# One transposition, one copy and one row transfer for two column groups of maxima

## The chip, the cores and the metric

The kernel runs on 1 core of one Trainium2 chip. The metric is device time in microseconds (us) of one launch. Before the change it is 2338.07 us, the median of three runs (2335.86 to 2340.33).

## The reference

The inputs are x (64 batches of 128 tokens, 512 wide), a context of 64 x 128 x 128, two gates and the weights of a mixture of experts. What is computed, with the expert part cut to a line:

```
q, k, v = layernorm(x), ctx, ctx            # 32 query heads of 16, 8 key/value heads, 4 query heads per key head
scores  = einsum('bkgsd,bktd->bkgst', qh, kh) / 4
weights = softmax(scores, axis=-1)
x = x + tanh(g_xattn) * (weights @ v)
x = x + tanh(g_ffn) * moe(layernorm(x))     # 32 experts, top 4, capacity 64, and a shared expert of 1408 columns
```

The change touches only the maximum that the softmax takes off each row of scores.

## The kernel before

Everything is written out by hand: five engine programs (PE, ACT, DVE, POOL, SP), each in its own order, tied by counting semaphores. The first stage is the attention. `iterations` runs a `body(B)` on every engine for B = 0 to 67; seven first and the last ones are written out, those between stand in a loop of two bodies. Each body has four steps, c = 0 to 3, one for a column group: eight query heads, four of each of two key heads.

A column group goes through these places. Batches are in flight together, so one step serves several of them:

- `q_cols` (PE, L623): four transpositions into `p_tq`; ACT copies them to `qt` (L425).
- First pass (PE, L704, `p_max`): the scores of group c of batch B, four matmuls. DVE reduces them over the keys to eight negated maxima per token in `negmax` (L562).
- Maxima (PE, L712): one transposition of `negmax` (128 x 8) into `p_mt` (8 x 128), ACT copies it to `mt` (L464), and SP sends it with two transfers, one per key head, into row 0 and row 64 of `qt` (L265), where it becomes one more term of the dot product. In the kernel before, this stands at the end of a step, behind the first pass, for the group of the step before: (B, c - 1), or (B - 1, 3) at c = 0. PE's step is: second pass, other work, `q_cols`, first pass, maxima.
- Second pass (PE, L663, `p_exp`): group c of batch B - 1 with the maxima's row in it, two matmuls, one step of the next body. It waits for the row's semaphore `mrow_in` and for the exponential before. ACT takes the exponential (L441).
- Then `pv` (PE, L639) at c = 2 (B - 1, first half) and c = 0 (B - 2, second half), its copy `pv_evac` (ACT, L430, `ot_sb`), the transpositions `o_cols` (L649), the division by the sums and the residual (DVE, L529, L542), a second layer norm (`xn`, L506), its transposition (PE, L673, `p_pv`, at c = 1 for B - 3), and router logits at c = 2 (L686).

`p_pv` is one bank used in turn by `pv`, by the transposed keys (`k_cols`, L615, at c = 3) and by the transposed `xn` (L673), so each of these waits until ACT has emptied it. SP's queue, in order, does the row transfers of every step, and between them at c = 0 the loads of `xres` and the store of `xn` rows, at c = 1 the loads of x and the context for B + 3, the values and the store of `xn` columns, at c = 2 the store of x2. In every second body SP also loads a slice of the shared expert's weights and ACT and POOL split it (`wgu_h`, L467, at the end of the even body; `wgu_l`, L402).

The second stage, from about 745 us on, is the mixture of experts and is not touched.

Of the kernel before, what the change touches and what calls it, by code (L numbers as in the profile page):

```python
# [14 lines left out]
F32 = mybir.dt.float32  # L15
F32R = mybir.dt.float32r
# [8 lines left out]
G = NH // NKV  # L25
# [73 lines left out]
def build(nc, x, ctx_in, g_xattn, g_ffn, Wr, Wg, Wu, Wd, Wsg, Wsu, Wsd, Wse, out):  # L99
# [7 lines left out]
    with stack:  # L107
# [29 lines left out]
        with ExitStack() as scope:  # L137
# [15 lines left out]
            xn = [sb(f"xn_{i}", [128, E]) for i in range(2)]  # L153
            xnT = [sb(f"xnT{i}", [128, KC, 128]) for i in range(2)]
            wr = sb("wr", [128, KC, NE + 1])
            negmax = [sb(f"negmax{i}", [128, 8]) for i in range(2)]
            mt = [sb(f"mt{i}", [8, 128], F32R) for i in range(2)]
            st1, st2 = sb("st1", [128, 6]), sb("st2", [128, 6])
            mv1 = [sb(f"mv1_{i}", [128, 2]) for i in range(2)]
            mv2 = [sb(f"mv2_{i}", [128, 2]) for i in range(2)]  # L160
# [18 lines left out]
            p_tq = ps("p_tq", [128, 512])  # L179
            p_pv = ps("p_pv", [128, 512])  # L180
            p_ot = ps("p_ot", [128, 512])
            p_mt = ps("p_mt", [8, 128])

            x_in = [sem(f"x_in{i}") for i in range(2)]
            kv_in = [sem(f"kv_in{i}") for i in range(2)]
# [53 lines left out]
            @block.sync  # L239
            def _(sp):  # L240
                sp.dma_start(wr[:, :, 0:NE], Wr.rearrange("(k p) e -> p k e", p=128)).then_inc(wr_in, 16)
                sp.dma_start(wr[:, :, NE:NE + 1], Wse.rearrange("(k p) e -> p k e", p=128),
                             allow_slow_non_contiguous=True).then_inc(wr_in, 16)
                sp.dma_start(gx[:, :], g_xattn.rearrange("(a n) -> a n", a=1).to_broadcast([128, 1])).then_inc(g_in, 16)
                sp.dma_start(gf[:, :], g_ffn.rearrange("(a n) -> a n", a=1).to_broadcast([128, 1])).then_inc(g_in, 16)

                def load_in(b):
                    wait(sp, qraw_done, b.n - 1)
                    sp.dma_start(xs[b.par][:, :], x_t[b.n]).then_inc(x_in[b.par], 16)
                    wait(sp, ks_done, b.n - 1)  # L250
                    sp.dma_start(kv[b.par][:, :], ctx_in[b.n]).then_inc(kv_in[b.par], 16)

                def body(B):
                    if isinstance(B.n, int) and B.n == 0:
                        load_in(B)
                        load_in(B + 1)
                        load_in(B + 2)
                    for c in range(NC):
                        m = (B - 1, 3) if c == 0 else (B, c - 1)
                        if m[0].ok:  # L260

                            b, cc = m
                            wait(sp, mt_done, 4 * b.n + cc + 1)
                            for g2 in range(2):
                                sp.dma_start(qt[b.par][64 * g2:64 * g2 + 1, cc, :].bitcast(F32),  # L265
                                             mt[cc % 2][4 * g2:4 * g2 + 4, :].bitcast(F32)).then_inc(mrow_in[cc % 2], 16)
                        if c == 0:
                            if (B - 1).ok:
                                wait(sp, x2_done, (B - 1).n - 1)
                                sp.dma_start(xres[(B - 1).par][:, :], x_t[(B - 1).n]).then_inc(xres_in[(B - 1).par], 16)  # L270
                            if (B - 3).ok:
                                b = B - 3
                                wait(sp, xn_done, b.n + 1)
                                sp.dma_start(xn_dram[bass.ts(b.n, 128), 0:E], xn[b.par][:, :]).then_inc(xn_out[b.par], 16)
                        if c == 1:
                            if (B + 3).ok:
                                load_in(B + 3)
                            if B.ok:
                                wait(sp, pv_mm, 2 * (B.n - 1))
                                if isinstance(B.n, int) and B.n < 2:  # L280
                                    sp.wait_ge(pads, 4)
                                sp.dma_start(vals[B.par][:, :, 0:D], ctx_in[B.n].rearrange("t (g d) -> t g d", d=D)).then_inc(v_in[B.par], 16)
                            if (B - 3).ok:
                                b = B - 3
                                wait(sp, xnT_done, b.n + 1)
                                alone(sp, spare_s)
                                sp.dma_start(xT_dram[:, :, bass.ts(b.n, 128)].rearrange("k p t -> p k t"), xnT[b.par][:, :, :]).then_inc(xnT_out[b.par], 16)
                        if c == 2 and (B - 2).ok:
                            b = B - 2
                            wait(sp, x2_done, b.n + 1)  # L290
                            sp.dma_start(out_rows[bass.ts(b.n, 128), :], x2[b.par][:, :]).then_inc(x2_out[b.par], 16)
                    if weights_load(B):

                        wait(sp, wlo_done, B.pair)
                        alone(sp, spare_s)
                        for w, src in enumerate((Wsg, Wsu)):
                            sp.dma_start(wst[:, w, :, :], src.rearrange("(k p) n -> p k n", p=128)[:, :, bass.ts(B.pair, WCH)]).then_inc(wst_in, 16)
                    if isinstance(B.n, int) and B.n == LAST:
                        for i in range(2):
                            sp.wait_ge(xnT_out[i], 32)  # L300
                        sp.dma_start(x_first[:, :, :], xT_dram[:, :, 0:TILE].rearrange("k p t -> p k t")).then_inc(x_first_in, 16)
                iterations(sp, body)
                sp.wait_ge(x_first_in, 16)
                for s in (x2_out, xn_out, xnT_out):
                    for i in range(2):
                        sp.wait_ge(s[i], 16 * (NB // 2))
# [102 lines left out]
            def _(act):  # L409
# [22 lines left out]
                def body(B):  # L432
# [3 lines left out]
                    for c in range(NC):  # L436
                        b = B - 1
                        if b.ok:
                            act.wait_ge(p2_mm, 4 * b.n + c + 1)
                            wait(act, pv_mm, 2 * (b.n - 1) + c // 2 + 1)  # L440
                            nc.scalar.activation(probs[c][:, :], p_exp[:, :, :].rearrange("p a b -> p (a b)"), ACT.Exp,  # L441
                                                 scale=float(D) ** -0.5).then_inc(exp_done, 1)
                        if c == 1 and (B - 3).ok:
                            b = B - 3
                            act.wait_ge(xnT_mm, b.n + 1)
                            wait(act, xnT_out[b.par], 16 * b.half)
                            wait(act, lg_mm, b.n - 1)
                            nc.scalar.activation(xnT[b.par][:, :, :].rearrange("p k t -> p (k t)"), p_pv[:, :], ACT.Copy).then_inc(xnT_done, 1)
# [7 lines left out]
                            q_evac(B, c + 1)  # L456
                        if c == 3 and (B + 1).ok:
                            q_evac(B + 1, 0)
                        b, cc = (B - 1, 3) if c == 0 else (B, c - 1)
                        if b.ok:  # L460

                            act.wait_ge(mt_mm, 4 * b.n + cc + 1)
                            wait(act, mrow_in[cc % 2], 32 * (2 * b.n + cc // 2))
                            nc.scalar.activation(mt[cc % 2][:, :], p_mt[:, :], ACT.Copy).then_inc(mt_done, 1)  # L464
                    if weights_split(B):
                        act.wait_ge(wst_in, 32 * (B.pair + 1))
                        nc.scalar.activation(w_cols(wgu_h, B.pair), wst_cols, ACT.Copy).then_inc(whi_done, 1)  # L467
# [3 lines left out]
            def _(dve):  # L471
# [59 lines left out]
                def body(B):  # L531
# [4 lines left out]
                    for c in range(NC):  # L536
# [21 lines left out]
                            x2_stats = stats(x2[B.par][:, :], st2)  # L558
                        if B.ok:
                            dve.wait_ge(p1_mm, 4 * B.n + c + 1)  # L560
                            wait(dve, mt_mm, 4 * B.n + c - 1)
                            nc.vector.tensor_reduce(negmax[c % 2][:, :].rearrange("p (g i) -> p i g", i=G),  # L562
                                                    p_max[:, :, :].rearrange("p a (h g t) -> p (a h) g t", g=2, t=128),
                                                    AX.X, ALU.max, negate=True).then_inc(max_done, 1)
                        if c == 0:
# [38 lines left out]
            def _(pe):  # L604
# [47 lines left out]
                def body(B):  # L652
# [3 lines left out]
                    for c in range(NC):  # L656
                        b = B - 1
                        if b.ok:

                            pe.wait_ge(mrow_in[c % 2], 32 * (2 * b.n + c // 2 + 1))  # L660
                            wait(pe, exp_done, 4 * b.n + c)
                            for g2 in range(2):
                                last = mm(p_exp[:, g2, :], kt[b.par][:, c, 128 * g2:128 * g2 + 128], qt[b.par][:, c, :],  # L663
# [27 lines left out]
                            o_cols(B - 2, 1)  # L691
                        if c == 3 and (B - 1).ok:
                            o_cols(B - 1, 0)
                        if c < 3 and B.ok:
                            q_cols(B, c + 1)
                        if c == 3 and (B + 1).ok:
                            q_cols(B + 1, 0)
                        if B.ok:
# [5 lines left out]
                                last = mm(p_max[:, i // 2, 256 * (i % 2):256 * (i % 2) + 256], qt[B.par][:, c, 128 * i:128 * i + 128],  # L704
                                          kt[B.par][:, c, :], start=True, stop=True)
                            last.then_inc(p1_mm, 1)
                        b, cc = (B - 1, 3) if c == 0 else (B, c - 1)
                        if b.ok:

                            pe.wait_ge(max_done, 4 * b.n + cc + 1)  # L710
                            wait(pe, mt_done, 4 * b.n + cc)
                            last = tr(p_mt[:, :], negmax[cc % 2][:, :], ident[:, :])  # L712
                            last.then_inc(mt_mm, 1)
                iterations(pe, body)


# [503 lines left out]
```

## Time and profile before

| what | value |
|---|---|
| median of three runs | 2338.07 us |
| the profiled execution's own time | 2336.49 us |
| its span (first to last instruction) | 2334.7 us |
| first stage | to about 745 us |
| PE busy, whole span | 98% |
| granted TensorE clock, mean | 0.996 |
| row transfers `qt<-mt` | 512, 2 KB each |

The span is what the profile's rows are measured in, from its first instruction; the execution's time is 1.8 us longer. In a timeline a row is: start, duration, engine, line, what is written from what, count, and in brackets the idle time before and who ended it. Matmuls are pipelined: each lasts longer than the distance to the next start, so the price of one is that distance and not its duration.

### The profile page before, as it was taken

Reading aid. Unit: us, or ns where it says so; the run is one execution under the profiler, and the core shown is the slowest. Engines: PE = TensorE matmul, PEld = TensorE weight load, DVE = VectorE, ACT = ScalarE, POOL = GpSimd, SP = SyncE. Lnnn points to the kernel's source line nnn. Section 1 sums busy time; section 2 is a strip of 40 time slices with the busy share of each in tenths; the row PEclk is TensorE's granted clock in tenths of the full one; section 3 lists DMA queues with packets and bytes.
Section 4 is the critical chain, followed back from the end, with each engine's and each line's share of the span. In section 5 each row is a group of like instructions: output and inputs, shape, how many; then the busy total and the mean of one; then the engine's idle time right before and its main releaser. Section 6 shows DMA issues by size and latency. Waiting matters only on the chain.

```text
span 2334.7 us, 41674 instructions
## 1 busy us (share of the span) xinstructions
PE 2298.7 (98%) x12545; PEld 1775.1 (76%) x12545; DVE 1159.6 (50%) x2218; ACT 799.2 (34%) x1440; POOL 595.6 (26%) x1395
## 2 busy tenths in 40 slices
PE   7999999999998999999999999999999999999999
PEld 5777777777775877787777877777777777777777
DVE  6999999999996842332222323233222232323232
ACT  6888888888885110110101101011010100101010
POOL 5677677667663100000000000000000000000100
PEclk9999999999998999999999999999999999999999
DMA  3555555545545132232222232212322123222411
GB/s 82 137 146 141 137 143 141 140 135 145 143 130 172 21 105 92 69 112 83 83 79 67 94 101 83 79 63 90 111 83 79 63 79 104 84 82 82 141 66 43
DMA packets 271248, 235.15 MB, mean 101 GB/s; under 512 B 122337, under 2 KB 198113, under 8 KB 271202
## 3 DMA queue, kind: packets, MB, share of 16 engines
q1 hardware_dynamic: 266850, 221.90, 31.6%
q0 software_dynamic: 4352, 12.65, 1.9%
q8 instruction: 27, 0.44, 0.1%
q14 instruction: 19, 0.16, 0.0%
HBM read 161.88 MB, written 71.57 MB: 100 GB/s over the span
## 4 chain that ended last, share of the span: by engine, by line
PE 67%; DVE 1%; DMA 0%; issue 0%; DVEq 0%; POOLq 0%
PE acc L1126 7%; PE p_u L1142 7%; PE p_u L1144 7%; PE p_u L1143 7%; PE acc L1127 7%; PE acc L1128 7%; PE p_g L1142 7%; PE p_g L1144 7%; PE p_g L1143 7%; PE p_x L1174 2%; PE p_y L1161 2%; PE p_x L1161 2%; PE p_x L1152 0%; DMA rows<-out_dram 0%; PE p_y L1167 0%; DVE rows L1106 0%
## 5 line engine op out<-in xcount | busy, mean ns | idle before, releaser
L1060 DVE TENSOR_TENSOR act_f<-p_u,act_f 128x512 f32<-128x512 f32 x176 | 121.7, 692 | 984.7 <-PE p_u L1144 984.6
L965 ACT ACTIVATE act_f<-p_g 128x512 f32<-128x512 f32 x176 | 105.3, 598 | 1215.9 <-PE p_g L1144 1194.8
L562 DVE TENSOR_REDUCE negmax<-p_max 128x8 f32<-128x1024 f32 x256 | 312.5, 1221 | 56.5 <-PE p_max L704 54.1
L1126 PE MATMUL acc<-wd_h,hh 128*128 128x512 f32 x704 | 279.9, 398 | 0.0
L1142 PE MATMUL p_u<-xh,wgu_h 128*128 128x512 f32 x704 | 274.5, 390 | 4.0 <-DVE act_f L1060 4.0
L1142 PE MATMUL p_g<-xh,wgu_h 128*128 128x512 f32 x704 | 276.0, 392 | 0.0
L1127 PE MATMUL acc<-wd_l,hh 128*128 128x512 f32 x704 | 274.7, 390 | 0.0
L1128 PE MATMUL acc<-wd_h,hl 128*128 128x512 f32 x704 | 274.7, 390 | 0.0
L1144 PE MATMUL p_g<-xh,wgu_l 128*128 128x512 f32 x704 | 274.5, 390 | 0.0
L1143 PE MATMUL p_g<-xl,wgu_h 128*128 128x512 f32 x704 | 274.4, 390 | 0.0
L1144 PE MATMUL p_u<-xh,wgu_l 128*128 128x512 f32 x704 | 274.4, 390 | 0.0
L1143 PE MATMUL p_u<-xl,wgu_h 128*128 128x512 f32 x704 | 274.3, 390 | 0.0
L441 ACT ACTIVATE probs<-p_exp 128x1024 f32<-128x1024 f32 x256 | 259.6, 1014 | 26.9 <-PE p_exp L663 17.2
L704 PE MATMUL p_max<-kt,qt 128*128 128x256 f32 x1024 | 185.1, 303 | 1.5 <-DVE negmax L562 1.5
L663 PE MATMUL p_exp<-qt,kt 128*128 128x512 f32 x512 | 182.5, 438 | 2.2 <-DMA qt<-mt 2.1
L425 ACT ACTIVATE qt<-p_tq 128x512 fp32r<-128x512 f32 x256 | 151.4, 591 | 59.5 <-PE p_tq L623 58.0
L1126 PEld LDWEIGHTS acc<-wd_h,hh 128*128 128x128 f32 x704 | 132.3, 188 | 47.5 <-DVE hl L1066 13.0
L623 PEld LDWEIGHTS p_tq<-ident,qs 128*128 128x128 f32 x1024 | 120.4, 147 | 58.8 <-ACT qt L425 45.3
L623 PE MATMUL p_tq<-ident,qs 128*128 128x128 f32 x1024 | 161.8, 281 | 2.8 <-POOL qs L364 1.8
L922 POOL DMA_INDIRECT eo<-out_dram,cur_tok x32 | 31.0, 968 | 504.6 <-DMA out_dram<-rows 408.1
L1142 PEld LDWEIGHTS p_u<-xh,wgu_h 128*128 128x128 f32 x704 | 132.2, 188 | 32.2 <-DVE act_f L1060 4.9
L1128 PEld LDWEIGHTS acc<-wd_h,hl 128*128 128x128 f32 x704 | 132.3, 188 | 27.9
(142 smaller groups left out, 3616.7 us busy)
## 6 DMA issues: line engine op xcount, KB each, us to landing
ew<-in_L_ffn_Wg_dram SPq DMA_DIRECT2D x32, 704.0 KB, 6.1
ew<-in_L_ffn_Wu_dram SPq DMA_DIRECT2D x32, 704.0 KB, 7.7
xs<-in_x_dram SPq DMA_DIRECT2D x64, 256.0 KB, 2.7
xres<-in_x_dram SPq DMA_DIRECT2D x64, 256.0 KB, 2.9
out_dram<-x SPq DMA_DIRECT2D x64, 256.0 KB, 2.0
xn_rows<-xn SPq DMA_DIRECT2D x64, 256.0 KB, 3.0
xn_cols<-xnT SPq DMA_DIRECT2D x64, 256.0 KB, 2.6
rows<-out_dram SPq DMA_DIRECT2D x16, 1024.0 KB, 5.2
```

The costliest lines, as they stand in the source:

```text
L425: nc.scalar.activation(qt[b.par][:, c, :], p_tq[:, :], ACT.Copy).then_inc(tq_done, 1)
L441: nc.scalar.activation(probs[c][:, :], p_exp[:, :, :].rearrange("p a b -> p (a b)"), ACT.Exp, scale=float(D) ** -0.5).then_inc(exp_done, 1)
L562: nc.vector.tensor_reduce(negmax[c % 2][:, :].rearrange("p (g i) -> p i g", i=G), p_max[:, :, :].rearrange("p a (h g t) -> p (a h) g t", g ...
L623: last = tr(p_tq[:, 128 * i:128 * i + 128], qs[b.par][:, c, i, :, :].rearrange("p g r -> p (g r)"), ident[:, :])
L663: last = mm(p_exp[:, g2, :], kt[b.par][:, c, 128 * g2:128 * g2 + 128], qt[b.par][:, c, :], start=True, stop=True)
L704: last = mm(p_max[:, i // 2, 256 * (i % 2):256 * (i % 2) + 256], qt[B.par][:, c, 128 * i:128 * i + 128], kt[B.par][:, c, :], start=True, s ...
L1126: mm(acc[:, j, :], a[:, t], wd_h[:, f, :], start=(f == 0), stop=False)
L1127: mm(acc[:, j, :], a[:, t], wd_l[:, f, :], start=False, stop=False)
L1128: last = mm(acc[:, j, :], b[:, t], wd_h[:, f, :], start=False, stop=(f == FC - 1))
L1142: mm(bank[:, :], wgu_h[:, w, k, cols], xh[:, k, :], start=(k == 0), stop=False)
L1143: mm(bank[:, :], wgu_h[:, w, k, cols], xl[:, k, :], start=False, stop=False)
L1144: last = mm(bank[:, :], wgu_l[:, w, k, cols], xh[:, k, :], start=False, stop=(k == KC - 1))
```

## The change

`negmax` and `mt` become 16 wide, one tile of them per half batch (two column groups, h = 0 or 1). The reduction of either group writes its eight maxima into its place in the same tile. One transposition, one copy and one transfer of 16 rows serve both groups. They stand at c = 2 for the half (B, 0) and at c = 0 for (B - 1, 1): on ACT directly behind the exponential and ahead of `pv_evac`, on PE behind `pv` (and the logits) and ahead of `q_cols` and the first pass. At c = 1 and c = 3 there is none. The second pass waits for a row at c = 0 and c = 2 only. SP's loads of x and the context for B + 3 move from c = 1 to c = 2, behind the row transfer.

```diff
-            negmax = [sb(f"negmax{i}", [128, 8]) for i in range(2)]
-            mt = [sb(f"mt{i}", [8, 128], F32R) for i in range(2)]
+            negmax = [sb(f"negmax{i}", [128, 16]) for i in range(2)]
+            mt = [sb(f"mt{i}", [16, 128], F32R) for i in range(2)]
...
-            p_mt = ps("p_mt", [8, 128])
+            p_mt = ps("p_mt", [16, 128])
... (SP)
-                        m = (B - 1, 3) if c == 0 else (B, c - 1)
-                        if m[0].ok:
+                        b, h = (B - 1, 1) if c == 0 else (B, 0)
+                        if c % 2 == 0 and b.ok:
...
-                            b, cc = m
-                            wait(sp, mt_done, 4 * b.n + cc + 1)
-                            for g2 in range(2):
-                                sp.dma_start(qt[b.par][64 * g2:64 * g2 + 1, cc, :].bitcast(F32),
-                                             mt[cc % 2][4 * g2:4 * g2 + 4, :].bitcast(F32)).then_inc(mrow_in[cc % 2], 16)
+                            wait(sp, mt_done, 2 * b.n + h + 1)
+                            sp.dma_start(qt[b.par][0:65:64, 2 * h:2 * h + 2, :].bitcast(F32),
+                                         mt[h][:, :].bitcast(F32)).then_inc(mrow_in[h], 16)
...
-                            if (B + 3).ok:
-                                load_in(B + 3)
...
+                        if c == 2 and (B + 3).ok:
+                            load_in(B + 3)
... (ACT: new place, behind the exponential; the old one at the end of the step is gone)
+                        b, h = (B - 1, 1) if c == 0 else (B, 0)
+                        if c % 2 == 0 and b.ok:
+                            act.wait_ge(mt_mm, 2 * b.n + h + 1)
+                            wait(act, mrow_in[h], 16 * b.n)
+                            nc.scalar.activation(mt[h][:, :], p_mt[:, :], ACT.Copy).then_inc(mt_done, 1)
... (DVE)
-                            wait(dve, mt_mm, 4 * B.n + c - 1)
-                            nc.vector.tensor_reduce(negmax[c % 2][:, :].rearrange("p (g i) -> p i g", i=G),
+                            if c % 2 == 0:
+                                wait(dve, mt_mm, 2 * (B.n - 1) + c // 2 + 1)
+                            nc.vector.tensor_reduce(negmax[c // 2][:, :].rearrange("p (g c i) -> p c i g", g=2, c=2)[:, c % 2, :, :],
... (PE, second pass)
-                            pe.wait_ge(mrow_in[c % 2], 32 * (2 * b.n + c // 2 + 1))
+                            if c % 2 == 0:
+                                pe.wait_ge(mrow_in[c // 2], 16 * (b.n + 1))
... (PE, new place, ahead of q_cols; the old one at the end of the step is gone)
+                        b, h = (B - 1, 1) if c == 0 else (B, 0)
+                        if c % 2 == 0 and b.ok:
+                            pe.wait_ge(max_done, 4 * b.n + 2 * h + 2)
+                            wait(pe, mt_done, 2 * b.n + h)
+                            last = tr(p_mt[:, :], negmax[h][:, :], ident[:, :])
+                            last.then_inc(mt_mm, 1)
```

## Rows read from the trace of the kernel before

**Rows 1.** The page: busy time of each engine with its share of the span.
```profile
PE 2298.7 (98%) x12545; PEld 1775.1 (76%) x12545; DVE 1159.6 (50%) x2218; ACT 799.2 (34%) x1440; POOL 595.6 (26%) x1395
```
**Rows 2.** Busy by window: stretch, length, PE, PEld, DVE, ACT, POOL, clock, DMA.
```profile
60.00:700.00 640.00, 637.90 (x4871) 469.85 (x4870) 592.30 (x1217) 562.44 (x1015) 447.02 (x1125) 1.00 0.52 140
```
**Rows 3.** Waits, 60 to 700 us: who waited for whom, total us, times, longest.
```profile
PEld p_pv L673 <- ACT ot_sb L430: 11.9, 26, 0.5
...
PE p_exp L663 <- DMA qt<-mt: 0.7, 1, 0.7
```
**Rows 4.** Timeline of PE, two bodies from 400 us.
```profile
400.44 0.63 PE L673 MATMUL p_pv<-ident,xn 128*128 128x128 f32 x4
...
411.39 0.60 PE L673 MATMUL p_pv<-ident,xn 128*128 128x128 f32 x4
...
412.62 0.71 PE L704 MATMUL p_max<-kt,qt 128*128 128x256 f32 x4
...
415.76 0.63 PE L623 MATMUL p_tq<-ident,qs 128*128 128x128 f32 x4
416.15 0.73 PE L704 MATMUL p_max<-kt,qt 128*128 128x256 f32 x4
416.71 0.27 PE L712 MATMUL p_mt<-ident,negmax 128*8 128x128 f32 x1
416.74 0.71 PE L663 MATMUL p_exp<-qt,kt 128*128 128x512 f32 x2
417.29 0.60 PE L615 MATMUL p_pv<-ident,ks 128*128 128x128 f32 x4
417.72 0.60 PE L649 MATMUL p_ot<-ident,ot_sb 128*128 128x128 f32 x4
...
418.51 0.71 PE L704 MATMUL p_max<-kt,qt 128*128 128x256 f32 x4
...
420.74 0.66 PE L623 MATMUL p_tq<-ident,qs 128*128 128x128 f32 x4
...
421.73 0.72 PE L663 MATMUL p_exp<-qt,kt 128*128 128x512 f32 x2
422.52 0.63 PE L673 MATMUL p_pv<-ident,xn 128*128 128x128 f32 x4
...
423.84 0.36 PE L704 MATMUL p_max<-kt,qt 128*128 128x256 f32 x1
```
**Rows 5.** The same timeline in a window that holds only the second `p_exp` matmul.
```profile
417.05 0.40 PE L663 MATMUL p_exp<-qt,kt 128*128 128x512 f32 x1
```
**Rows 6.** Timeline of ACT in the same bodies.
```profile
417.02 0.27 ACT L464 ACTIVATE mt<-p_mt 8x128 fp32r<-8x128 f32 x1
...
420.11 0.25 ACT L464 ACTIVATE mt<-p_mt 8x128 fp32r<-8x128 f32 x1
...
421.56 0.57 ACT L430 ACTIVATE ot_sb<-p_pv 128x512 f32<-128x512 f32 x1
```
**Rows 7.** Timeline of DVE in the same bodies.
```profile
411.14 1.21 DVE L562 TENSOR_REDUCE negmax<-p_max 128x8 f32<-128x1024 f32 x1
...
419.27 1.23 DVE L562 TENSOR_REDUCE negmax<-p_max 128x8 f32<-128x1024 f32 x1 [0.61 <-PE p_max L704]
...
422.48 1.21 DVE L562 TENSOR_REDUCE negmax<-p_max 128x8 f32<-128x1024 f32 x1
```
**Rows 8.** The `kv` load (128 pieces of 512 bytes), 60 to 700 us: issue to landing.
```profile
DMA to landing us min/median/max: 2.0/2.3/4.1
```
**Rows 9.** Timeline of SP where a row came late: start, issue time, transfers.
```profile
87.22 1.21 SPq L265 DMA_DIRECT2D qt<-mt  x2
```
**Rows 10.** PE in the same place.
```profile
91.00 0.72 PE L663 MATMUL p_exp<-qt,kt 128*128 128x512 f32 x2 [0.70 <-DMA qt<-mt]
```
**Rows 11.** Timeline of PE where the stage runs out.
```profile
720.06 0.27 PE L712 MATMUL p_mt<-ident,negmax 128*8 128x128 f32 x1
...
722.25 0.70 PE L663 MATMUL p_exp<-qt,kt 128*128 128x512 f32 x2
```

More of the change, by code:

```diff
@@ L458, in body @@
                             q_evac(B + 1, 0)
[L459 to L464, printed above, removed]
                     if weights_split(B):
@@ L706, in body @@
                             last.then_inc(p1_mm, 1)
[L707 to L713, printed above, removed]
                 iterations(pe, body)
```

## The prediction, made before the changed kernel ran

> **What bounds the kernel now.** The page first: PE is busy for 98% of the span [rows 1]. Then the windows, because the change lies in the first stage alone: from 60 to 700 us PE is busy 637.9 of 640 us at a granted clock of 1.00, DVE 592, ACT 562 [rows 2]. So PE's own instructions set the time, and DVE and ACT are close enough behind to matter. Last the timeline of two bodies, where such a "busy" is to be doubted: a matmul's recorded length hides short stalls. From one transposition of `xn` to the next PE takes 10.95 us (400.44 to 411.39), then 11.13 us (411.39 to 422.52) [rows 4]. The longer one is the body in which ACT splits a slice of weights. There the two `p_exp` matmuls are followed by L673 only 0.79 us after their start (421.73 to 422.52), against 0.55 in the neighbour that waits for nothing (416.74 to 417.29) [rows 4], and the waits name the reason: L673 on ACT's copy `ot_sb`, 26 times of some 29 such bodies [rows 3]. So one body in two is held 0.24 us by ACT, the other runs at PE's pace.
>
> **What a transposition of maxima is worth on PE.** Its recorded 0.27 us is no price. Start to start it takes 0.03 (416.71 to 416.74), but then the first `p_exp` matmul takes 0.31 to the second (417.05 [rows 5]), which itself takes 0.24 to the next instruction (417.29) [rows 4, 5]. So 0.34 for the transposition and the first, less 0.24 for a matmul like it: 0.10. Four transpositions of the same 128 columns take 0.43 (417.29 to 417.72), 0.108 each [rows 4]. Bounds: 0.03 by the starts alone, 0.27 by its length; I take 0.108. Of four a batch two go: 0.216 a batch, and 128 in the stage. Eight more columns of `negmax` don't lengthen it: the 128 columns of the identity are what is streamed. The two that stay only change places.
>
> **What holds that gain back.** The time from c = 3 of one body to c = 1 of the next has two other chains.
> - ACT, in the body with the split: exponential, two key copies, `q_evac`, [maxima copy], weight slice, exponential, `pv_evac`, whose start at 421.56 lets L673 go [rows 4, 6]. The change takes the copy of 420.11 out (0.25 us [rows 6]) and puts one like it in behind the exponential of c = 0, ahead of `pv_evac`. The chain keeps its length, so of the two transpositions removed per body the one at the end of c = 3 only turns into a longer wait at L673 (0.24 becomes about 0.35). Left: 0.108 for these bodies.
> - DVE, in the other: the reduction of group 0 ends at 412.35 (411.14 + 1.21) and the first pass of group 1 starts at 412.62, 0.27 later [rows 4, 7]. In the split body it is 423.69 and 423.84, 0.15, which I read as the shortest handover [rows 4, 7]. So 0.12 is free and 0.108 is asked for: it fits, just. I take 0.20 instead of 0.216.
> - The moved transposition at c = 0 needs the reduction of group 3, which ends at 420.50 (419.27 + 1.23); with 0.12 to 0.15 for the handover it can start at 420.62 to 420.65. PE would come to that place at 420.63 (420.74, where L623 starts now, less the transposition gone from the end of c = 3) [rows 4, 7]. 0 to 0.03 us of stall a batch; this is why I take 0.20.
>
> **The row's way, now shorter in time.** Before, each group's row had about two and a half steps; now a half's transposition starts where L623 starts at c = 2 (415.76) or c = 0 (420.74), and its row is needed two steps on. For the first half, PE from there: transposition 0.11, L623 and first pass 0.95, then the whole of c = 3, 2.22 (416.74 to 418.51, another first pass of 0.56 as from 416.15 to 416.71, less the transposition): 3.3 us [rows 4]. The way: ACT starts its copy 0.31 after the transposition starts (416.71 to 417.02), copies 0.27 [rows 4, 6], SP, idle by then, issues at once (it has finished with the `xn` columns), and the transfer lands. How long a 16-row transfer takes no row shows. The nearest is the `kv` load with pieces of the same size: 2.0 at least, 2.3 in the middle, 4.1 at worst [rows 8]. With 2.3 it lands at 2.9 of 3.3: hidden, with 0.4 to spare. For the second half the sum is the same, but in split bodies ACT comes to the copy only at about 421.31 (421.56 less a copy), 0.4 later than the transposition would let it (420.63 + 0.31) [rows 4, 6], and L673's own wait of 0.35 gives most of that back. Above 2.7 us of transfer PE waits at the second pass. The longest case on the page, where the row's two transfers were issued at 87.22 and 87.82 and PE got its row at 91.00, is 3.2 us behind the second issue, with a 256 KB store ahead in the queues [rows 9, 10].
>
> The Trainium skill ("DMA: Bandwidth & Descriptors", section "Why a DMA increments its semaphore by 16 and not by 1") speaks against the new form: a transfer is spread over the largest number of engines, up to 16, that divides the slowest dimension of both sides. The destination's is now 2 (rows 0 and 64) and the source's 16, so two engines would carry eight pieces each, one behind the other. `kv` also has eight pieces per engine if it uses all sixteen, so by this rule too the row lands at some 2.9 us of 3.3; spread over sixteen engines it would be earlier, and no row here shows how many a transfer used.
>
> **Costs I put at nothing.** SP: eight issues of 0.6 us a batch (1.21 for two [rows 9]) become two; SP is never what PE waits for except once in 640 us [rows 3], so this frees time that nobody lacks. The loads of x and the context go out behind the row transfer of c = 2, 1 us later than now, and are used a body later; 11 us of cover. On ACT at c = 2 `pv_evac` now stands behind a copy that waits for PE's transposition: it ends at about 1.15 us after that starts (0.31, 0.27, 0.57), and `k_cols`, which reuses the bank, wants it at 1.6 (0.11, 0.95, 0.55) [rows 4, 6]; beyond that 0.45 it would cost what is missing. ACT's two copies less a batch lie in its idle time except as told above.
>
> **Ends.** Where the stage runs out there is no first pass to cover the row: the last transposition at 720.06 needs 2.9 us to its row, and the second pass of group 2 stands at 722.25 [rows 11]: up to 0.7 us of waiting, I take 0.5. In the first bodies PE is not yet the bound: four bodies at 0.1.
>
> **Sum.** 29 split bodies by 0.108 is 3.1, 29 others by 0.20 is 5.8, the beginning 0.4, the end -0.5: 8.8 us. The profiled execution (2334.7 of span, 2336.49 in all) would be 2327.7; it lies 1.6 below the median 2338.07, from which the forecast is 2329.3, say 2329.5.
>
> **Rivals.**
> - *The row comes late* (slower). The 16-row transfer takes not 2.3 but 2.9 us, between the `kv` median and the 3.2 of the congested case. The second pass then waits about 0.2 us at c = 0 and at c = 2; less 0.15 gained that is 0.25 a batch, 58 times: +14, 2352 us. For it: the slack is 0.4 and the transfer's form is new. Against: one wait for a row in 640 us although these rows queue behind long stores now [rows 3]. It decides from 2.7 us on.
> - *Nothing to be seen.* A transposition costs the 0.03 us between starts, because its streaming lies under its neighbours': 128 of them are 3.8 us, less 0.5 to 1 at the ends: 2335 us. Against: the first `p_exp` is longer behind it by the difference [rows 4, 5]. The same time results if the ACT and DVE chains hold all bodies.
> - *All of it.* The holds go too, because ACT and DVE come earlier than I think: 0.216 in 60 bodies, 13 us: 2325 us. For it: the ACT copies gone; against: the chain in the split body keeps its two copies.
>
> **Chances.** Forecast 0.50, late rows 0.14, nothing 0.20, all of it 0.16. What this kernel's measurement can tell from no change is about 0.2%, 4.7 us. Faster by more: nearly all of the first, all of the last, little of the third: 0.67. Within it: 0.20. Slower: 0.13. The forecast's own range is 2326 to 2333; for 8 in 10 it goes from 2322 (all of it, with some of the 0.24 us wait as well) to 2340 (the rows a little late).
>
> **What would show it.** PE's distance from L673 to L673 falls from 10.95 and 11.13 to about 10.75 and 11.0; at c = 1 and c = 3 the second pass follows the first pass directly. L673's waits for `ot_sb` stay or grow. No wait of the second pass on `qt<-mt` beyond one or two: many of them, 0.1 us or more, mean the late row. If the distances fall by less than 0.05 the price of a transposition was wrong; if the new L712 waits for `negmax` by more than 0.05 at c = 0, the DVE handover was.

## The result and the profile after

The changed kernel takes 2321.65 us (median of four runs, 2320.48 to 2323.45), the kernel before 2336.97 (four runs): a ratio of 0.993, 95% interval 0.992 to 0.9947. That is 15.3 us less; forecast was 8.6 less than the 2338.07, and the time lies just below the stated range (2322 to 2340). The profiled execution has a span of 2319.0 us against 2334.7.

The page and the window of the steady stage, in the columns of [rows 1] and [rows 2]; PE is as full as before, over a shorter time:

```profile
PE 2281.3 (98%) x12417; PEld 1760.4 (76%) x12417; DVE 1154.4 (50%) x2218; ACT 763.7 (33%) x1312; POOL 594.0 (26%) x1395
```
```profile
60.00:690.00 630.00, 628.67 (x4791) 461.92 (x4790) 591.61 (x1226) 533.53 (x905) 449.40 (x1134) 1.00 0.54 145
```

The waits there answer to [rows 3]. `L673`'s wait is still there and shorter, and there is one wait for a row:

```profile
PEld p_pv L673 <- ACT ot_sb L428: 8.8, 27, 0.4
...
PEld p_exp L663 <- DMA qt<-mt: 0.3, 1, 0.3
```

PE's timeline, answering to [rows 4]. From one transposition of `xn` to the next, 404.22 to 415.03, ACT splits a weight slice (`wgu_h` at 412.78); in the text below such a body is a split body. Its step c = 0, from 411.80, is also the first behind the turn of the loop of two bodies:

```profile
404.22 0.60 PE L673 MATMUL p_pv<-ident,xn 128*128 128x128 f32 x4
...
408.46 0.27 PE L699 MATMUL p_mt<-ident,negmax 128*16 128x128 f32 x1
408.57 0.60 PE L622 MATMUL p_tq<-ident,qs 128*128 128x128 f32 x4
408.93 0.72 PE L711 MATMUL p_max<-kt,qt 128*128 128x256 f32 x4
409.49 0.63 PE L663 MATMUL p_exp<-qt,kt 128*128 128x512 f32 x2
409.95 0.60 PE L614 MATMUL p_pv<-ident,ks 128*128 128x128 f32 x4
...
411.18 0.72 PE L711 MATMUL p_max<-kt,qt 128*128 128x256 f32 x4
411.80 0.73 PE L663 MATMUL p_exp<-qt,kt 128*128 128x512 f32 x2
412.45 1.06 PE L638 MATMUL p_pv<-probs,vals 128*32 128x512 f32 x8
413.45 0.28 PE L699 MATMUL p_mt<-ident,negmax 128*16 128x128 f32 x1
413.56 0.60 PE L622 MATMUL p_tq<-ident,qs 128*128 128x128 f32 x4
413.92 0.72 PE L711 MATMUL p_max<-kt,qt 128*128 128x256 f32 x4
414.47 0.62 PE L663 MATMUL p_exp<-qt,kt 128*128 128x512 f32 x2
415.03 0.63 PE L673 MATMUL p_pv<-ident,xn 128*128 128x128 f32 x4
```

What to see: without a transposition ahead of them the two `p_exp` matmuls take 0.46 to the next instruction (409.49 to 409.95) where transposition and pair took 0.58 (416.71 to 417.29 [rows 4]). The new transposition takes 0.11 (408.46 to 408.57), and the `q_cols` behind it 0.36 (408.57 to 408.93), where they took 0.39 behind the logits (415.76 to 416.15 [rows 4]). And at c = 0 the `p_exp` pair takes 0.65 to `pv` (411.80 to 412.45), not 0.55.

The same distances as means over 23 pairs of bodies, worked out from single starts in the two traces. A pair is a split body and one without a split; "removed" and "added" are the transpositions of maxima:

| stretch on PE, us per pair of bodies | before | after | difference |
|---|---|---|---|
| first pass of c = 1 to `pv` of c = 2 (a transposition removed) | 2.441 | 2.215 | -0.226 |
| first pass of c = 2 to `k_cols` (removed) | 2.277 | 2.050 | -0.227 |
| first pass of c = 3 to `pv` of c = 0 (removed) | 2.450 | 2.493 | +0.043 |
| first pass of c = 0 to L673 (removed) | 2.481 | 2.127 | -0.354 |
| logits to first pass of c = 2 (one added) | 0.780 | 0.934 | +0.154 |
| `pv` to first pass of c = 0 (one added) | 0.826 | 0.938 | +0.112 |
| everything | 22.07 | 21.57 | -0.50 |

29.5 pairs of 0.50 are 14.8 us of the 15.7 by which the spans differ; the last microsecond is at the stage's ends.

### The profile page after: what moved, and what is told of

Read it like the earlier page. It is cut to its first block, busy times and chain, and to the rows that moved or that the text cites. A ratio compares the mean times of both kernels' runs of the same rounds, so it can differ in the third digit from the quotient of the medians.

```text
span 2319.0 us, 40286 instructions
## 1 busy us (share of the span) xinstructions
PE 2281.3 (98%) x12417; PEld 1760.4 (76%) x12417; DVE 1154.4 (50%) x2218; ACT 763.7 (33%) x1312; POOL 594.0 (26%) x1395
## 4 chain that ended last, share of the span: by engine, by line
PE 67%; DVE 1%; DMA 0%; issue 0%; DVEq 0%; POOLq 0%
PE acc L1126 7%; PE p_u L1142 7%; PE p_u L1144 7%; PE p_u L1143 7%; PE acc L1128 7%; PE acc L1127 7%; PE p_g L1142 7%; PE p_g L1144 7%; PE p_g L1143 7%; PE p_x L1174 2%; PE p_y L1161 2%; PE p_x L1161 2%; PE p_x L1152 0%; DMA rows<-out_dram 0%; PE p_y L1167 0%; DVE rows L1106 0%
## 5 line engine op out<-in xcount | busy, mean ns | idle before, releaser
L663 PE MATMUL p_exp<-qt,kt 128*128 128x512 f32 x512 | 163.5, 401 | 0.2
L622 PE MATMUL p_tq<-ident,qs 128*128 128x128 f32 x1024 | 155.8, 275 | 2.6 <-POOL qs L362 1.8
L1144 PEld LDWEIGHTS p_g<-xh,wgu_l 128*128 128x128 f32 x704 | 132.2, 188 | 27.6
L1144 PEld LDWEIGHTS p_u<-xh,wgu_l 128*128 128x128 f32 x704 | 132.2, 188 | 27.4
```

Source lines behind the costliest of these rows:

```text
L622: last = tr(p_tq[:, 128 * i:128 * i + 128], qs[b.par][:, c, i, :, :].rearrange("p g r -> p (g r)"), ident[:, :])
L1144: last = mm(bank[:, :], wgu_l[:, w, k, cols], xh[:, k, :], start=False, stop=(k == KC - 1))
```

## Experiments

Each ran on the same chip as runs of the kernel before (its medians there 2335.4 to 2337.2). "Changed" is the changed kernel's 2321.6. It was not run again beside the experiments, so a difference of 2 or 3 us from it says little by itself; the small effects are read from distances on PE. Those are medians of starts over the steady bodies of each trace.

**Only the transfers.** The kernel before, one transfer per group:

```diff
-                            for g2 in range(2):
-                                sp.dma_start(qt[b.par][64 * g2:64 * g2 + 1, cc, :] ...
+                            sp.dma_start(qt[b.par][0:65:64, cc, :].bitcast(F32), mt[cc % 2][:, :].bitcast(F32)) ...
+                        if c == 2 and (B + 3).ok:      # was c == 1
+                            load_in(B + 3)
```

> The kernel before with only SP's side of the change: one transfer per column group instead of two (rows 0 and 64 in one), and the loads for B + 3 behind the row transfer of c = 2. Transpositions and copies stay four a batch. Theory: SP's queue was not what PE waited for, so 2337 us, within 2. Rival, that half of the gain came from a relieved queue: 2330 us.

Measured 2336.59, ratio 0.9999 (0.999 to 1.0008), and every distance of the table as before to 0.003 us. SP's side is worth nothing.

**An idle transposition at c = 3, and at c = 1.** The changed kernel with, behind the first pass:

```diff
+                        if c == 3 and B.ok:            # the other kernel: c == 1, 2 * B.n
+                            wait(pe, mt_done, 2 * B.n + 1)
+                            tr(p_mt[:, :], ident[:, 0:16], ident[:, :])
```

> The changed kernel with one idle transposition (16 columns of the identity into the bank of the maxima, read by nobody) behind the first pass at c = 3, where the change took one away. Theory: the pv matmuls of c = 0 wait there for ACT's second key copy (L417 ends 0.14 to 0.19 us before them in both kernels), so the transposition taken away at c = 3 gave nothing, and the idle one costs nothing: 2321.6 us, within 1.5. Rival, every transposition is worth its 0.108 us: 64 times 0.108 is 7 us, 2328.5 us.

> The changed kernel with the idle transposition behind the first pass at c = 1 instead of c = 3. Theory: nothing holds PE behind it (the second pass and pv of c = 2 follow at their shortest distance), so here it costs its full 0.108 us a batch, 64 times: 7 us, 2328.5 us. Rival, that idle transpositions cost nothing anywhere, as at c = 3 (2323.0): 2323 us.

Measured 2323.04 at c = 3 and 2329.03 at c = 1: 1.4 and 7.4 us more than changed. So a transposition is worth its 0.11 us where nothing holds PE behind it, and next to nothing at c = 3: what the change removed there gave next to nothing.

The trace of the kernel with the idle one at c = 3 says why, and differs by body. Where no turn of the loop lies between, first pass to `pv` takes 1.225 with it and 1.220 without (400.94 to 402.16 below). In the split body, behind the turn (411.61 to 412.95), the stretch takes 1.339 with it and 1.272 without, and L673's wait behind it shrinks by the same 0.07:

```profile
400.94 0.72 PE L711 MATMUL p_max<-kt,qt 128*128 128x256 f32 x4
401.50 0.27 PE L716 MATMUL p_mt<-ident 128*16 128x128 f32 x1
401.52 0.71 PE L663 MATMUL p_exp<-qt,kt 128*128 128x512 f32 x2
402.16 1.06 PE L638 MATMUL p_pv<-probs,vals 128*32 128x512 f32 x8
...
411.61 0.72 PE L711 MATMUL p_max<-kt,qt 128*128 128x256 f32 x4
412.17 0.27 PE L716 MATMUL p_mt<-ident 128*16 128x128 f32 x1
412.29 0.73 PE L663 MATMUL p_exp<-qt,kt 128*128 128x512 f32 x2
412.95 1.06 PE L638 MATMUL p_pv<-probs,vals 128*32 128x512 f32 x8
```

**Without the second key copy.** What holds `pv` at c = 0 (the second head of each pair keeps zero keys, its scores are left out):

```diff
-                    nc.scalar.activation(kt[b.par][64:128, :, 128:256], p_pv[64:128, :] ..., ACT.Copy).then_inc(kt_done, 1)
```

> The changed kernel without the second of ACT's two key copies (L417; the second head of each pair keeps zero keys, so that part of the scores is left out); the first copy releases pv. Theory: pv at c = 0 no longer waits for ACT and follows the second pass after 0.56 instead of 0.66 us; the transposition of maxima behind it then waits for DVE's reduction of group 3 by up to 0.03. With ACT 0.6 us earlier, the weight slice comes earlier too and POOL's low part misses DVE's xn, so that L673's wait (0.085 in every second body) goes as well: 0.08 a body and 0.085 in every second, 7 to 8 us, 2314 us. Rival, that PE's own instructions or the loop's turn make the 0.66: 2321.6 us, within 2.

Measured 2315.20. In the body without a split `p_exp` to `pv` at c = 0 falls from 0.666 to 0.553, and L673's wait is gone in the split body (0.550 to 0.469). But there `p_exp` to `pv` stays at 0.656, and first pass to `p_exp` before it at 0.608:

```profile
408.51 0.71 PE L710 MATMUL p_max<-kt,qt 128*128 128x256 f32 x4
409.12 0.73 PE L662 MATMUL p_exp<-qt,kt 128*128 128x512 f32 x2
409.78 1.07 PE L637 MATMUL p_pv<-probs,vals 128*32 128x512 f32 x8
...
419.25 0.72 PE L710 MATMUL p_max<-kt,qt 128*128 128x256 f32 x4
419.80 0.62 PE L662 MATMUL p_exp<-qt,kt 128*128 128x512 f32 x2
420.35 1.06 PE L637 MATMUL p_pv<-probs,vals 128*32 128x512 f32 x8
```

So ACT's key copies are the hold in one body, and something else is in the other. Where the hold is gone, part of the gain is lost again one step on: `pv` to the transposition becomes 1.008 (it then starts 0.134 behind the end of DVE's reduction), and `q_cols` to the first pass becomes 0.407 instead of 0.356, which was not taken apart. The split body's c = 0 is the first step behind the turn of the loop of two bodies, and that was tried next, with the same part left out:

```diff
-                with eng.Fori((FIRST - 1) // 2, (LAST - 1) // 2) as pair:
+                with eng.Fori((FIRST - 1) // 2, (LAST - 1) // 2, 2) as pair:
...
+                    body(Batch(pair + 1, 1))
+                    body(Batch(pair + 1, 2))
```

> The kernel without the second key copy (that part of the scores is left out), with a loop of four bodies instead of two (13 turns instead of 27). There the second pass and pv of c = 0 followed at 0.554 and 0.553 us in one body and at 0.608 and 0.656 in the other, whose c = 0 is the first step behind the loop's turn. Theory: the 0.16 is the turn's; in the body that no longer has a turn ahead of it the distances become 0.554 and 0.553, and the median 14 times 0.16, 2 us lower, 2313. Rival, that the weight slice's ACT or POOL work makes it: both even bodies keep 0.608 and 0.656.

Measured 2314.29 (two runs only), and the long distance now comes in every fourth body only: first pass to `p_exp` to `pv` is 0.555 and 0.553 three times, then 0.561 and 0.656. The split body that has no turn ahead of it is short, so the split is not the cause and the excess goes with the turn. But only 0.11 of it does here, against 0.16 with two bodies to a turn: the 0.05 ahead of `p_exp` is nearly gone although a turn still stands there. It is also gone in the kernel with the idle transposition at c = 1 (1.215 from first pass to `pv` behind the turn, 1.272 without it). The loops of all five engines turn at this place and were changed together, so the runs don't show in which engine the time goes.

**Why L673's wait fell.** In the split body its start follows the end of DVE's `xn` by 0.255 us in both kernels (in 26 of 27 and 26 of 28 such bodies to 0.003), while its distance to the end of `ot_sb` is 0.37 before and 0.23 after. DVE and POOL of the kernel before, to be read beside L673 at 422.52 [rows 4]:

```profile
421.10 1.16 DVE L506 TENSOR_SCALAR xn<-x,mv,rs 128x512 f32<-128x512 f32 x1
```
```profile
421.02 0.95 POOL L402 TENSOR_TENSOR wgu_l<-wst,wgu_h 128x352 f32 x1 [0.81 <-ACT wgu_h L467]
```

And after, beside L673 at 415.03:

```profile
413.77 1.00 DVE L504 TENSOR_SCALAR xn<-x,mv,rs 128x512 f32<-128x512 f32 x1
```
```profile
413.54 0.94 POOL L400 TENSOR_TENSOR wgu_l<-wst,wgu_h 128x352 f32 x1 [0.41 <-ACT wgu_h L465]
```

`xn` takes 0.54 us in the body where POOL has no `wgu_l` beside it. POOL starts `wgu_l` 0.08 us ahead of `xn` before and 0.23 ahead after, because ACT's `wgu_h` no longer stands behind a copy of maxima. "Stretched" is more exactly "held": `xn` ends 0.28 us behind the end of `wgu_l` (0.280 to 0.293 in every split body of both kernels), wherever `wgu_l` began, so each 0.1 us by which `wgu_l` comes earlier lets `xn` end 0.1 earlier. Three kernels test this. The first is the kernel before with `wgu_l` behind `k_stacks` of the next body (POOL), nothing else:

> The kernel before with POOL's low part of the weight slice (wgu_l) moved from the end of the even body to behind k_stacks of the next, so that it no longer runs while DVE normalises x2 (xn, L506). Theory: PE's transposition of xn (L673) waits in every second body for DVE's xn, which POOL's operation at the same time stretches from 0.54 to 1.14 us; it would be short again and the 0.24 us of waiting gone: 29 times 0.24 is 7 us, less what the stretched reduction or qraw costs: 2330 to 2333 us. Rival, the reading of the prediction, that ACT's copy ot_sb holds L673: ACT's order is unchanged, so 2337 us and the distance of 11.1 us stays.

Measured 2338.73, ratio 1.0011 (1.0002 to 1.002): no gain, outside the 2330 to 2333 expected, but the trace confirms who held L673. `xn` is 0.54 again, and `p_exp` to L673 falls from 0.771 to 0.551 although ACT's order is untouched. The time comes back a few instructions later: `wgu_l` now runs beside `is_top`, the reduction starts later and the first pass waits (`q_cols` to first pass 0.778 instead of 0.419):

```profile
422.81 0.54 DVE L508 TENSOR_SCALAR xn<-x,mv,rs 128x512 f32<-128x512 f32 x1
423.27 1.04 DVE L600 TENSOR_TENSOR is_top<-iota_e,idx_f 128x128 f32<-128x128 f32 x1
```
```profile
423.93 0.60 PE L675 MATMUL p_pv<-ident,xn 128*128 128x128 f32 x4
...
425.59 0.59 PE L706 MATMUL p_max<-kt,qt 128*128 128x256 f32 x3 [0.19 <-DVE negmax L564]
```

The second gives ACT an idle copy back, where the copy of maxima stood (`nc.scalar.activation(idle[:, :], ident[0:16, :], ACT.Copy)` ahead of `wgu_h`):

> The changed kernel with an idle ACT copy (16 x 128, identity to a scratch tile that nobody reads) at the end of every body, where the copy of the maxima stood before the change, ahead of the weight slice's high part (wgu_h). Theory: L673's wait in every second body fell from 0.24 to 0.085 because wgu_h, and with it POOL's wgu_l, comes 0.15 us earlier without that copy and overlaps DVE's xn less. With the idle copy xn is 1.14 us again instead of 1.00 and the wait 0.22: 29 times 0.15 is 4.4 us, 2326 us. Rival, that the wait fell for another reason (PE's own order): 2321.6 within 1.5, and xn stays at 1.00.

Measured 2327.78, 6.1 above changed (4.4 expected). `p_exp` to L673 in the split body is 0.740 (0.550 without the idle copy, 0.771 before) and no other distance moves by more than 0.003. So the copy that left ACT at c = 3 is what shortened this wait. By which way this kernel alone can't say, since the idle copy lies on `ot_sb`'s chain too (L673 starts 0.22 behind its end here); the kernels before and behind this one, where ACT's order is untouched, show that it is POOL's. The third puts `wgu_l` under a reduction, in the changed kernel, one body later:

```diff
+                    if B.off == 2 and (not isinstance(B.pair, int) or 1 <= B.pair <= NB // 2):   # POOL, behind k_stacks
+                        pool.wait_ge(whi_done, B.pair)
+                        nc.gpsimd.tensor_tensor(w_cols(wgu_l, B.pair - 1), ...).then_inc(wlo_done, 1)
...
+                        if c == 1 and weights_split(B):                                          # SP: load of the slice
```

> A version meant to be used: the changed kernel with POOL's low part of the weight slice moved to the next even body, between k_stacks and q_stacks, where POOL is idle for 2 us and DVE runs a reduction from PSUM, and SP's load of the slice to c = 1 of the even body. Theory: POOL's operation stretches DVE's operations on SBUF (xn 0.54 to 1.0 or 1.14, is_top 0.37 to 1.04 us) but not the reduction; then L673 waits in no body (0.085 in every second) and the first pass of group 1 neither (0.06): 29 times 0.17 is 5 us, 2316.5 us. Rival, that the reduction is stretched too: no gain, 2321 us or more.

Measured 2318.77, ratio to before 0.993 (0.9913 to 0.9947). That is 2.9 below changed by the medians, but the changed kernel's ratio is 0.993 too, so the times don't show a gain; the steady part of the trace does. L673 waits in no body (0.464 and 0.468), nor does the first pass of group 1 but for single bodies at the stage's ends, and a pair of bodies takes 21.41 us instead of 21.57. Here `wgu_l` and the reduction run side by side and neither is longer:

```profile
403.14 1.23 DVE L563 TENSOR_REDUCE negmax<-p_max 128x8 f32<-128x1024 f32 x1
```
```profile
403.00 0.98 POOL L393 TENSOR_TENSOR wgu_l<-wst,wgu_h 128x352 f32 x1
```

To this version a hint for the loop's closing branch was added (`hint_back_edge=True`):

> The version with POOL's low part under the reduction (2318.8 us) with, in addition, each engine's loop-closing branch announced at the top of the iteration. Theory: where the 0.05 us a turn at c = 0 (second pass at 0.609 instead of 0.555) is the fetch behind the branch, it goes: 27 times 0.05 is 1.4 us, 2317.5 us; the key copies still hold pv. Rival, that it is the work of the counters and not the fetch: 2318.8 us, or more for the added instruction.

Measured 2321.57: no gain. First pass to `p_exp` behind the turn became 0.712 instead of 0.608. So the hint doesn't cure that wait, and what in the turn takes the time stays open.

**The place on PE.** The changed kernel with the transposition behind `q_cols`:

> The changed kernel with the one transposition of a half batch behind q_cols instead of ahead of it (still ahead of the first pass). Theory, from the two traces: ahead of q_cols it fills a start-up gap that the first transposition of q_cols has behind pv (0.057 us) and behind the logits (0.034 us), so its price there is about 0.055 and 0.075 us and not 0.11. Behind q_cols the gaps come back: 0.09 us a batch, 5.5 us, about 2327 us where the changed kernel has 2321.6. Rival, that the place is worth nothing and the extra gain is due to fewer copies and transfers: 2321.6, within 1.5.

Measured 2342.48, 21 us above changed and slower than before (1.0026, 1.0016 to 1.0036): far from both the theory and its rival. ACT's copy of the maxima, ahead of `pv_evac`, waited longer for PE (104.6 us in the window, 68.7 in the changed kernel), and PE's next users of the bank waited for `pv_evac` in all bodies:

```profile
ACT mt L446 <- PE p_mt L703: 104.6, 85, 1.6
...
PEld p_pv L614 <- ACT ot_sb L428: 22.3, 54, 0.4
PEld p_pv L673 <- ACT ot_sb L428: 20.9, 54, 0.5
```

The same with ACT's copy behind `pv_evac`:

> As the kernel with the transposition behind q_cols (2342.5 us), but ACT's copy of the maxima stands behind pv_evac instead of ahead of it. Theory: of the 21 us which that place cost, 5.5 were the start-up gaps of q_cols behind pv and the logits, and the rest was pv_evac, held behind a copy that waits for the late transposition, which held the key transpositions (c = 3) and those of xn (c = 1). With pv_evac ahead only the gaps remain: 2327 us, up to 2330 if a row lands late. Rival, that the place itself costs all of it (the reduction, the row): 2340 us.

Measured 2324.12: 2.5 above changed by the medians, 3.8 by the pair of bodies (0.13 longer). The gaps of `q_cols` do come back (transposition and `q_cols` 0.500 and 0.521 instead of 0.467 and 0.469, 0.085 a body), but in split bodies L673's wait shrinks by 0.046 to fill part of it. So the place ahead of `q_cols` is worth some 3 us, and the other 18 us or so of the kernel above were the order on ACT.

## Why the prediction was wrong

The direction, the price of a transposition on PE and the cover of the row were right; the gain was put 6.7 us too small. Two steps failed that made it so, and a third that hid part of their error. By steps, in us per pair of bodies, where the forecast had -0.31 and the traces have -0.50:

- *The price of a transposition*, 0.108: right. 0.113 where it was removed at c = 1 and c = 2, 7.4 us for 64 idle ones at c = 1. The rival "nothing to be seen" is refuted.
- *"The two that stay only change places"*: failed, 0.166 too dear. As the next two errors nearly cancel, the miss in time comes from this step. Ahead of `q_cols` the two cost 0.077 and 0.056, not 0.108: they stand in a gap that `q_cols` had behind the logits and `pv`. This could have been read before: at c = 2 `q_cols` took 0.39 to the instruction behind it (415.76 to 416.15 [rows 4]) and takes 0.36 behind a transposition (408.57 to 408.93).
- *The hold at L673 is ACT's chain, whose length stays, so the wait grows to 0.35*: failed, 0.25 too pessimistic. The prediction followed the name in the waits [rows 3] and did not compare the ends: `ot_sb` ended 0.39 ahead of L673, `xn` 0.26. The holder was DVE's `xn`, itself held by POOL's `wgu_l`, and that in turn hung on the ACT copy that the change took away. The wait fell from 0.24 to 0.085 instead of growing.
- *A chain that was missed*, 0.26 too good: `pv` at c = 0 waits for the second key copy, which in the kernel before ended 0.150 us ahead of `pv` in both bodies, just not late. The transposition removed at c = 3 gave 0.005 in the body without a split, where the key copy is shown to hold. In the split body the stretch became 0.047 longer (1.225 to 1.272), which goes with the loop's turn; why the kernel before loses nothing at its turn is not known. The transposition that stood there is not the reason by itself: with the idle one in its place the turn still costs 0.11. The list of waits names the key copy 27 times, with the same numbers before and after, so it doesn't tell that the copy began to cost anything:

```profile
PEld p_pv L639 <- ACT kt L419: 9.9, 27, 0.4
```
```profile
PEld p_pv L638 <- ACT kt L417: 9.9, 27, 0.4
```
- *DVE's handover at c = 0, 0 to 0.03 of stall*: not tested by the change itself. `pv` to the transposition is 0.997, as `pv` to `q_cols` was, but only because `pv` came later than forecast. Without the second key copy it is 1.008, a stall of 0.01: right in size.
- *The row*: right in sum. Its transfer is issued 0.69 us behind the start of the transposition (408.46 to 409.15) and the second pass starts at 411.80 without a wait for it; the landing records have it at 410.87, 1.7 us behind the issue, less than the 2.3 of `kv`. The rival "the row comes late" is refuted: one wait of 0.3 us in 630.
- *The ends*: +0.4 and -0.5 forecast, some +1 measured, not taken apart.

The two big errors about holds nearly cancel (0.25 too pessimistic, 0.26 too optimistic), which is luck: with the first alone the forecast would have missed by about twice as much. What is left is the cheap place of the added transpositions, 29.5 times 0.166 or 4.9 us, and the ends. The rival "all of it" came nearest in time (2325), but not by its mechanism: the removal at c = 3 gave nothing.

## What to carry to other kernels

Before naming who holds an instruction, compare its start with the ends of all that it waits for, over several bodies and in both kernels: the one whose distance stays the same is the first suspect, whatever the wait list says. It is a suspect and no proof: `pv` stood a constant 0.150 behind the key copy in the kernel before, where the copy cost nothing. An experiment that moves only the suspect decides. Price an added instruction by the gap that it may fill, and look at the instruction behind it, not at itself. When an instruction leaves one engine's queue, look what then starts earlier on the others, and whom that runs beside.

## What the runs showed of the hardware

- A POOL `tensor_tensor` of 128 x 352 (0.94 us) holds DVE operations on SBUF that start beside it until it is done: `xn` takes up to 1.19 us instead of 0.54 and ends 0.28 behind POOL's end, `is_top` takes 1.04 instead of 0.37 and ends 0.15 behind. It leaves DVE's reduction from PSUM at 1.23.
- One transfer of 16 rows of 512 bytes into two partitions takes 0.54 us to issue, no more than one of 4 rows (0.59). Its semaphore gets two late increments (410.86 and 410.87) where a 128-row load gets sixteen. That agrees with what the Trainium skill says ("DMA: Bandwidth & Descriptors", "Why a DMA increments its semaphore by 16 and not by 1"): each engine that a transfer uses adds one when its data is in, and their number is the largest up to 16 that divides the slowest dimension of both sides, here 2. The row was no later for it: 1.7 us from issue to the last increment (median of 117), 1.64 for the second of two 4-row transfers before (421.20 to 422.85).
- A transposition of 128 columns costs 0.11 us in a stream, and 0.06 to 0.08 where it fills the gap that the next group would have had.
- Behind the turn of the loops, first pass to `pv` takes 0.16 us longer than in the other body without the second key copy (1.265 against 1.108), and 0.11 with four bodies to a turn. Where the key copy holds the other body anyway, the turn adds 0.05 in the changed kernel (1.272 against 1.220), 0.15 with the hint, 0.11 with an idle transposition there, and nothing in the kernel before (1.225 in both). What makes the difference is open.
